# Second context attention: four row groups of scores at once, values a batch later, context loads behind the first gathers

## The reference

```python
    scale = 1.0 / jnp.sqrt(jnp.sqrt(jnp.float32(d)))
    q = x.reshape(B, T, H, d) * scale          # x is layer-normed; d = 16, H = 16
    k = cond_k.reshape(B, S, H, d) * scale     # cond_k = cond_v = ctx, S = 256
    w = jax.nn.softmax(jnp.einsum('bthd,bshd->bhts', q, k), axis=-1)
    out = jnp.einsum('bhts,bshd->bthd', w, v).reshape(B, T, W)
    return out @ w_proj.T + b_proj
```

## Time and profile before

| | |
|---|---|
| runs | 967.45 us median (965.89 to 968.01) |
| profiled execution, in all | 957.07 us |
| its span, first to last instruction | 955.2 us |
| mean granted TensorE clock | 0.909 |
| stage a2 in the trace | 667 to 802 us |
| PE busy over the span | 823.5 us (86%) |
| DVE, ACT, POOL busy | 586.8, 422.4, 329.7 us |

### The profile page before, as it was taken

How to read it: one execution, slowest core, us unless ns; L and a number is a source line. 1 busy time by engine, 2 the same in 40 slices (tenths; PEclk the granted TensorE clock), 3 DMA queues, 4 the chain that set the end, 5 groups by cost and what they waited for, 6 DMA issues and landing times. The chain is left out here.

```text
span 955.2 us, 20462 instructions
## 1 busy us (share of the span) xinstructions
PE 823.5 (86%) x7532; PEld 631.2 (66%) x7532; DVE 586.8 (61%) x1436; ACT 422.4 (44%) x1243; POOL 329.7 (35%) x465
## 2 busy tenths in 40 slices
PE   5999998898999999958787399998388996867897
PEld 4888887455999999834465388887266774465335
DVE  3555565446999999873495623223578787455474
ACT  3665655446654442023554210000257664555562
POOL 2112211113999999610051260100643332233001
PEclk9999999788999999875988599999589998979899
DMA  7112600000000000000001036532645210000001
GB/s 245 32 24 73 228 24 2 2 0 1 1 1 2 1 1 1 1 0 0 1 2 45 22 120 184 192 112 78 192 116 167 78 60 2 1 3 2 0 1 46
DMA packets 41846, 49.32 MB, mean 52 GB/s; under 512 B 7090, under 2 KB 37268, under 8 KB 41492
## 3 DMA queue, kind: packets, MB, share of 16 engines
q1 hardware_dynamic: 37204, 40.93, 13.4%
q0 software_dynamic: 1536, 4.20, 1.5%
q10 hardware_dynamic: 3008, 2.88, 0.9%
HBM read 43.81 MB, written 4.19 MB: 50 GB/s over the span
## 5 line engine op out<-in xcount | busy, mean ns | idle before, releaser
L723 POOL TENSOR_TENSOR r_faded<-r_state,rec_f 128x256 f32<-128x256 f32 x128 | 82.1, 642 | 19.8 <-DVE r_state L705 9.7
L751 PE MATMUL r_u_ps<-r_t_in,l_same_head 128*128 128x256 f32 x256 | 87.2, 422 | 0.1
L729 POOL TENSOR_TENSOR r_q_in<-r_state,rec_q 128x256 f32<-128x256 f32 x128 | 82.0, 641 | 0.3 <-DVE r_state L702 0.2
L758 PEld LDWEIGHTS r_o_ps<-l_head_of,r_q_in 128*128 128x128 f32 x512 | 77.0, 191 | 6.9 <-POOL r_q_in L729 0.4
L1428 ACT ACTIVATE a_prob<-a_s_ps,a_negmax 128x256 f32<-128x256 f32 x128 | 59.0, 488 | 38.3 <-DVE a_negmax L1465 38.2
L1088 ACT ACTIVATE a_prob<-a_s_ps,a_negmax 128x256 f32<-128x256 f32 x128 | 59.1, 486 | 19.0 <-DVE a_negmax L1144 19.0
L758 PE MATMUL r_o_ps<-l_head_of,r_q_in 128*128 128x8 f32 x512 | 65.2, 236 | 0.3 <-POOL r_q_in L729 0.3
L1651 POOL TENSOR_TENSOR a_prob<-a_prob,a_rden 128x512 f32<-128x512 f32 x32 | 32.3, 1042 | 84.5 <-DVE a_rden L1712 84.5
L1977 PE MATMUL m_h_ps<-m_rowsT,l_w 128*128 128x256 f32 x256 | 57.3, 383 | 0.0
L702 DVE TENSOR_TENSOR r_state<-r_update,r_faded 128x256 f32<-128x256 f32 x128 | 54.3, 424 | 4.4
L691 DVE TENSOR_TENSOR r_t_in<-r_state,r_par_ps 128x256 f32<-128x256 f32 x128 | 53.7, 420 | 5.3
(11 more groups left out here) (344 smaller groups left out, 1934.2 us busy)
## 6 DMA issues: line engine op xcount, KB each, us to landing
l_w<-in_B_w SPq DMA_DIRECT2D x16, 1024.0 KB, 5.6
a_ctxT<-in_ctxT SPq DMA_DIRECT2D x31, 256.0 KB, 2.8
a_ctx<-in_ctx SPq DMA_DIRECT2D x16, 256.0 KB, 3.6
expert_out<-m_y ACTq DMA_DIRECT2D x7, 256.0 KB, 5.7
all_X<-in_x SPq DMA_DIRECT2D x4, 256.0 KB, 5.6
l_b<-in_B_b SPq DMA_DIRECT2D x1, 1024.0 KB
routed_rows<-ffn_xn SPq DMA_DIRECT2D x8, 128.0 KB, 1.8
l_F_up<-in_F_up SPq DMA_DIRECT2D x1, 1024.0 KB, 6.1
```

Of the source, the lines that this page charges most:

```text
L723: nc.gpsimd.tensor_tensor(faded[m][:, :, :], state[(t + 1) % 2][m][:, :, :], row("f", t, m), ALU.mult).then_inc(faded_ready[m], 1)
L729: nc.gpsimd.tensor_tensor(q_in[t % 2][m][:, :, :], state[t % 2][m][:, :, :], row("q", t, m), ALU.mult).then_inc(q_ready[m], 1)
L751: nc.tensor.matmul(u_ps[t % 2][m][:, 0:B, :], same_head[:, :], t_in[m][:, :, :], start=False, stop=True).then_inc(u_mm[m], 1)
L758: mm = nc.tensor.matmul(o_ps[:, 2 * m + c, :, t % U], q_in[t % 2][m][:, c * (B // 2):(c + 1) * (B // 2), :], head_of[:, :], start=True, st ...
```

## The change

The scores of a batch become one group of 16 instructions over all four row groups, issued when all exponentials of the batch before are done. On PE the loop body for batch n becomes: scores(n+1), transposes 2 and 3 of n, values(n-1), output (odd n), the turn, transposes 0 and 1 of n+1. The list `uses` follows. ScalarE empties the banks of r = 0 and 1 before the next batch's exponentials; DVE those of r = 2 and 3, between and behind the maxima of the next batch, with heads and add behind them.

At the start, SP sends only the first `ctxT` and then waits for the first four combinings (`used`) before any other context load. The first queries are made by DVE straight from the turned bank in PSUM, four instructions (`first_queries`), instead of by POOL from `QT`; POOL issues the gathers 8 to 11 at once. DVE combines tile 2 ahead of the first queries and tile 3 behind them, takes the maxima of batch 0, then norms tiles 2 and 3 and lays out the values of batches 0 and 1 (`lay_out`). In the diff, lines without a change are left out where they don't help.

```diff
@@ -1230,7 +1230,7 @@
         normed = Normed(nc, sc, "x", X, eps, keep=sc.sb("x_rows", [P, NT, D]))
-        used, turned, turned_taken, first_values = (sc.sem(n) for n in ("used", "turned", "turned_taken", "first_values"))
+        used, turned, turned_taken, first_values, first_q = (sc.sem(n) for n in ("used", "turned", "turned_taken", "first_values", "first_q"))
         s_ps = [sc.ps(f"s_ps{r}", [P, KD, S]) for r in range(4)]
@@ -1244,17 +1244,18 @@
 
-            return (pt_act, ONE + n + 1) if r == 3 else (pt_dve, ONE + 3 * n + r + 1)
-        uses = [(("turned", 0), (turned_taken, ONE + 1))]
+            return (pt_act, ONE + 2 * n + r + 1) if r < 2 else (pt_dve, ONE + 2 * n + r - 1)
+        uses = [(("turned", 0), (turned_taken, ONE + 1))] + [((0, r), transposed(0, r)) for r in (0, 1)]
         for n in range(B):
-            for r in range(4):
-                uses.append(((n, r), transposed(n, r)))
-                if r == 1 and n % 2 == 1 and n > 1:
-                    uses.append((("out", n // 2 - 1), (x_added, ONE + n // 2)))
-                if r == 1 and n in TURNED_BESIDE:
-                    uses.append((("turned", TURNED_BESIDE[n]), (turned_taken, ONE + TURNED_BESIDE[n] + 1)))
+            uses += [((n, r), transposed(n, r)) for r in (2, 3)]
+            if n % 2 == 1 and n > 1:
+                uses.append((("out", n // 2 - 1), (x_added, ONE + n // 2)))
+            if n in TURNED_BESIDE:
+                uses.append((("turned", TURNED_BESIDE[n]), (turned_taken, ONE + TURNED_BESIDE[n] + 1)))
+            if n + 1 < B:
+                uses += [((n + 1, r), transposed(n + 1, r)) for r in (0, 1)]
         uses.append((("out", NT - 1), (x_added, ONE + NT)))
@@ -1274,6 +1275,8 @@
                     sp.dma_start(ctxT[n % NB][:, :, :], ctxT_d[n].rearrange("(k p) s -> p k s", p=P)).then_inc(ctxT_in[n % NB], 16)
+                    if n == 0:
+                        sp.wait_ge(used, ONE + 4)
                     if n >= NB:
@@ -1319,7 +1322,6 @@
                     gather(n)
-                queries(0)
                 for n in range(8, 12):
@@ -1338,19 +1340,20 @@
                     u = place[what]
+                    if u == 3:
+                        pe.wait_ge(first_q, ONE + 2 * KD)
                     if u >= 3:
...
 
-                def scores(n, h):
+                def scores(n):
                     t, j = n // 2, n % 2
-                    if h == 0:
-                        pe.wait_ge(q_ready, ONE + 2 * t + 2)
-                        pe.wait_ge(*loaded(ctxT_in, n))
+                    pe.wait_ge(*((q_ready, ONE + 2 * t) if t >= 1 else (first_q, ONE + 2 * KD)))
+                    pe.wait_ge(*loaded(ctxT_in, n))
                     if n >= 1:
-                        pe.wait_ge(exp_done, ONE + 4 * (n - 1) + 2 * h + 2)
+                        pe.wait_ge(exp_done, ONE + 4 * n)
                     for m in range(KD):
-                        for r in (2 * h, 2 * h + 1):
+                        for r in range(4):
                             rows = slice(32 * r, 32 * r + 32)
@@ -1369,7 +1372,7 @@
                         pe.wait_ge(heads_ready, ONE + t)
-                    for r in (2, 3):
+                    for r in (1, 3):
                         pe.wait_ge(*transposed(n, r))
@@ -1398,23 +1401,23 @@
                 turn(0)
-                scores(0, 0)
-                scores(0, 1)
+                scores(0)
+                transposes(0, 0)
+                transposes(0, 1)
                 for n in range(B):
-                    transposes(n, 0)
+                    if n + 1 < B:
+                        scores(n + 1)
+                    transposes(n, 2)
+                    transposes(n, 3)
                     if n >= 1:
                         values(n - 1)
-                    transposes(n, 1)
                     if n % 2 == 1 and n > 1:
...
                     if n + 1 < B:
-                        scores(n + 1, 0)
-                    transposes(n, 2)
-                    transposes(n, 3)
-                    if n + 1 < B:
-                        scores(n + 1, 1)
+                        transposes(n + 1, 0)
+                        transposes(n + 1, 1)
                 values(B - 1)
@@ -1436,6 +1439,8 @@
                     act.wait_ge(turned, ONE + c + 1)
+                    if c == 0:
+                        act.wait_ge(first_q, ONE + 2 * KD)
                     nc.scalar.activation(QT[:, :, c * 2 * P:(c + 1) * 2 * P], bank(("turned", c))[:, :].rearrange("p (k q) -> p k q", k=KD), ACT.Copy).then_inc(turned_taken, 1)
@@ -1444,14 +1449,13 @@
                 for n in range(B):
+                    for r in (0, 1):
+                        take_transposed(n, r)
                     if n + 1 < B:
-                        exps(n + 1, 0)
+                        for r in range(4):
+                            exps(n + 1, r)
                     if n in TURNED_BESIDE:
                         take_turned(TURNED_BESIDE[n])
-                    take_transposed(n, 3)
-                    if n + 1 < B:
-                        for r in range(1, 4):
-                            exps(n + 1, r)
                     if n == 3:
@@ -1503,35 +1507,47 @@
 
+                def lay_out(n):
+                    dve.wait_ge(*loaded(ctx_in, n))
+                    for e in range(2):
+                        nc.vector.tensor_copy(vals[n][:, e, :, :, e * HD:(e + 1) * HD], ctx[n][:, :, :].rearrange("p c (i e d) -> p c i e d", e=2, d=HD)[:, :, :, e, :]).then_inc(first_values, 1)
+                def first_queries():
+                    dve.wait_ge(turned, ONE + 1)
+                    for e in range(2):
+                        for k in range(KD):
+                            nc.vector.tensor_scalar(qpair[0][:, k, :, e, :], bank(("turned", 0))[:, 2 * k * P:(2 * k + 1) * P].rearrange("p (j q) -> p j q", j=2), par_q[:, e:e + 1], None, ALU.mult).then_inc(first_q, 1)
                 for j in range(2):
...
                 dve.wait_ge(zeroed, ONE + 2)
-                for n in range(2):
-                    dve.wait_ge(*loaded(ctx_in, n))
-                    for e in range(2):
-                        nc.vector.tensor_copy(vals[n][:, e, :, :, e * HD:(e + 1) * HD], ctx[n][:, :, :].rearrange("p c (i e d) -> p c i e d", e=2, d=HD)[:, :, :, e, :]).then_inc(first_values, 1)
-                for c in range(2):
-                    combine(2 * c)
-                    combine(2 * c + 1)
-                    normed.variances(dve, c)
-                    scale_tiles(c)
+                combine(0)
+                combine(1)
+                normed.variances(dve, 0)
+                scale_tiles(0)
+                combine(2)
+                first_queries()
+                combine(3)
+                normed.variances(dve, 1)
                 for r in range(4):
                     maxima(0, r)
+                scale_tiles(1)
+                lay_out(0)
+                lay_out(1)
                 for n in range(B):
-                    take_transposed(n, 0)
-                    if n >= 2 and n % 2 == 0:
-                        heads(n // 2 - 1)
-                    take_transposed(n, 1)
                     if n + 1 < B:
...
                         maxima(n + 1, 1)
-                    if n >= 3 and n % 2 == 1:
-                        add(n // 2 - 1)
                     take_transposed(n, 2)
-                    reciprocals(n)
                     if n + 1 < B:
...
                         maxima(n + 1, 3)
+                    take_transposed(n, 3)
+                    reciprocals(n)
+                    if n >= 2 and n % 2 == 0:
+                        heads(n // 2 - 1)
+                    if n >= 3 and n % 2 == 1:
+                        add(n // 2 - 1)
                     if n in (1, 2):
```

## The result

The changed kernel takes 951.18 us (median of 4 runs, 946.9 to 954.09), the kernel before beside it 966.79: ratio 0.984 with the interval 0.9815 to 0.9864, a gain of 15.6 us. The forecast was 956.9 with 953 to 964: the sign and the mechanism held, and the gain was larger than forecast. Three later measurements of such a pair, on three chips, gave 12.3 us (e5), 11.4 (e14) and 13.7 (e18).

A forecast was written before the change was run, and what follows sets the result against it. TensorE was taken to bound the later batches of the second context attention. Terms -6.8, -1.6, -3.35 and +1.2 summed to -10.55 us, taken off the 967.45 median to give 956.9, range 953 to 964.

The forecast's parts named there:

- 2, to the end of batch 0's exponentials: Stage start: batch 0's exponentials end at 688.4 instead of 689.96, -1.6 us (bounds +1.0 to -3.2).
- 4, tail: Stage end: batch 14's values and output 6 now also follow the last exponential, +1.2 us (0 to +2.4).
- the softmax loop: Steady batches: scores, maximum and eight exponentials through three engines bound each batch, sum 5.69 us, taken as 5.70.
- Rival A: Small gain: near-ties in the loop break, 6.0 instead of 5.7, start gives nothing; -3 to -7, 962 us; chance 0.24.
- rival D: Four row groups don't run together in this stage: scores 2.1, loop 6.75, sum +3, 970 us; chance 0.03.
- rival B: Larger gain: gathers land in 2.8 us throughout, tail costs nothing; -13.4, 954 us; chance 0.08.
- Rival C: Batch loop: TensorE idling drops the clock to 1.2 GHz, TensorE binds again; slower, 988 us; chance 0.06.
- Term 1: Batches 6 to 15: eight steps of 5.70 and two turned-tile steps of 6.65, 58.9 against 65.7 us, -6.8.
- Term 3: Batches 1 to 5: 36.75 against 40.1 us, -3.35, with the clock rise left at 699.
- if it rises at once, -1 to -2: Batches 1 to 5: an immediate clock rise would shorten them by a further 1 to 2 us.

The follow-up runs named there:

- e5: The changed kernel, unchanged, timed again beside the kernel before: 948.97 us beside 961.3, ratio 0.9867.
- e14: The changed kernel, unchanged, timed again in a pair with e13: 950.65 us, ratio 0.9876 to the kernel before.
- e18: The changed kernel, unchanged, timed again in a pair with e17: 947.43 us, ratio 0.9878 to the kernel before.
- e1: The kernel before, unchanged, timed and profiled again: 960.77 us beside 960.71, ratio 0.9993.
- e13: The kernel before, unchanged, timed and profiled again: 961.38 us beside 962.03, ratio 0.9994.
- e17: The kernel before, unchanged, timed and profiled again: 961.41 us beside 961.12, ratio 0.9998.
- e2: The changed kernel's batch loop with the start of the kernel before: 946.56 us beside 960.71 for the kernel before, ratio 0.986.
- e9: The changed kernel with scores cut into two halves of two row groups, a transposed group between: 956.75 us beside 966.5 for the kernel before, ratio 0.9899.
- e12: The changed kernel plus unread identity products, 43 ahead of the first turned tile, 17 behind the first scores: 952.14 us beside 966.5, ratio 0.9849.
- e11: The kernel before plus unread identity products, 50 ahead of the first turned tile, 10 behind the first scores: 966.53 us beside 966.5, ratio 1.0001.
- e10: The changed kernel with combinings spread over the first batches, gathers 12 to 15 earlier, batch 14's values moved forward: 947.59 us, ratio 0.9812 to the kernel before.
- e15: As e10 (spread combinings, earlier gathers, moved values), but without the hold of the context loads: 944.84 us beside 962.03 for the kernel before, ratio 0.9822.
- e8: The changed kernel plus unread identity products, 40 ahead of the first turned tile, 30 behind the first scores: 947.8 us beside 961.3, ratio 0.9866.
- e6: The changed kernel with its 16 score instructions ordered by row group: 947.24 us, ratio 0.9845 to the kernel before.

## Why the prediction was wrong in size

The stage by the prediction's terms, from the four profiles of each kernel unchanged (before: the first, e1, e13, e17; after: the first, e5, e14, e18):

| term | before, us | after, us | difference of means | first pair | forecast |
|---|---|---|---|---|---|
| 2, to the end of batch 0's exponentials | 21.93, 22.35, 22.63, 22.03 | 20.38, 21.00, 21.14, 21.57 | -1.2 | -1.55 | -1.6 |
| 3, batches 1 to 5 | 40.10, 40.68, 40.58, 39.59 | 38.04, 35.83, 35.82, 35.83 | -3.9 | -2.06 | -3.35 |
| 1, batches 6 to 15 | 65.73, 67.27, 67.27, 67.28 | 58.08, 59.66, 59.60, 58.09 | -8.0 | -7.65 | -6.8 |
| 4, tail | 6.51, 7.29, 7.37, 6.51 | 7.92, 7.92, 7.92, 7.91 | +1.0 | +1.41 | +1.2 |
| stage | 134.27, 137.59, 137.85, 135.41 | 124.42, 124.41, 124.48, 123.40 | -12.1 | -9.85 | -10.55 |

**Right.** The mechanism and its bound: the softmax loop of 5.77 us (5.70), the 16 scores in 1.08, TensorE idle in front of them. Rival A's ties cost nothing in this loop, rival D is refuted by each profile of the changed kernel, and of rival B neither cause held (the tail costs 1.0 to 1.4, and the exponentials of batch 0 gained 1.2 to 1.6). Rival C's fall of the clock came only as the single dips above, at most 1.6 us a stage in the changed kernel's four profiles. The steps forecast for batches 3 to 5, 7.3, 8.2 and 7.85, are 7.63, 7.88 and 7.84 (batch 3 of the first profile apart).

**Wrong, small.** Term 1: I gave two batches with a turned tile 6.65, for a wait of TensorE on the bank that the add frees. After's rows at batch 7, on PE and DVE:

```profile
734.84 1.04 PE L1367 MATMUL a_w_ps<-all_ident,a_prob 128*128 128x128 f32 x8
735.81 1.15 PE L1358 MATMUL a_s_ps<-a_ctxT,a_qpair 32*128 32x256 f32 x16
```

```profile
734.70 0.37 DVE L1494 TENSOR_TENSOR all_X<-a_w_ps,all_X 128x256 f32<-128x256 f32 x1
```

The add ends 5.35 us behind the last exponential before (729.72), not 5.6, and the transposes run through beside it: those steps are 5.98, TensorE's own work, 0.67 less each, 1.3 together; the eight others are 5.77 instead of 5.70, 0.5 more. Term 3: the clock rises about a batch earlier than I put it, so that step 2 is 5.76 and not 6.7; that was the prediction's own side condition ("if it rises at once, -1 to -2"). It stood in no case's sum.

**The step that failed.** "The median of the timed runs is 967.45, 10.4 longer than the profiled one; nothing says the difference lies in this stage, so I take the gain off it." Part of it does lie there. The first profile's stage of 134.27 is the shortest of four; the others are 1.1 to 3.6 us longer, at stretches with a granted clock under 1.00 around batch 6 or 7 and, in e1 and e13, at a later rise (step 2: 9.47 and 9.38 against 8.91 and, in e17, 8.02) and the tail (7.29 and 7.37 against 6.51, at a clock of 0.85 and 0.84 there). The old loop has TensorE as its bound in most of batches 6 to 15 and paid 1.5 us for its dip in each of the three later profiles; the changed kernel paid as much in e5 and e14 and nothing in the other two. So the change takes away more than one undisturbed execution shows: 12.1 us on the mean of four, where the sum from one gave 10.55. The kernel before accounts for 2.0 of that difference (mean 136.28 against 134.27), less 0.5 by which the changed one is longer than forecast (124.18 against 123.72). The pairs on a chip agree with it in time on average, though each is up to 2 us off: stage -13.4 and 11.4 us timed (e13, e14), -12.0 and 13.7 (e17, e18), -14.2 and 14.2 (e1, and e2 with the loop alone).

Of the 5.7 us between forecast and result, that is 1.5; 0.7 is the kernel before, at 966.79 in the second measurement instead of 967.45; the other 3.5 are the 15.6 us of the first measurement against 12.1. The interval of those 15.6 begins at 13.1 (966.79 x (1 - 0.9864)), so 2.5 of the 3.5 may be noise. They stay open. The kernel before took 966.5 to 966.8 us in two measurements (the first, and that of e9 to e12) and 960.7 to 962.0 in the four others, and idle times that nothing released stand in profiles of those two. For their costing the old order more: e11, the kernel before but for its added products, loses some 6 us to them in step 2, where the changed kernel lost 2.2 in its first profile and e12 0.7, in the values of the same batch; and with e11's stage as the old order's, e9 and e12 come out by stage as they do by time. Against its being all of it: nearly the same kernels gained 18.9 us there (e10) and 17.2 elsewhere (e15), 14.4 there (e12) and 13.5 elsewhere (e8), so 1 to 2 us more. It is not shown: there is no profile of the unchanged kernel before from a measurement in which its profile, too, took 966 us.

## What to carry to other kernels

Before a forecast from one profile is set on the median, ask whether the two differ, and let the sum have a term for it where the changed stage is bound by the engine whose clock varies. A change that takes TensorE off the path takes off what its clock costs only where another engine covers it: here batch 5 at 0.78 cost nothing, batches 6 and 7 still 1.5 us. When an engine is relieved, work out the next loop through the other engines link by link; here three links read from rows and one estimated gave 5.69 for a measured 5.77. And look for the last engine that has several pieces in a row where the others wait: spreading four combinings took 3.7 us off two steps, while the whole rearranged start gave nothing measurable.

## What the runs showed of the hardware

- The order within the 16 score instructions over four row groups doesn't matter: 1.08 us with the groups taken in turn, 1.10 with four of one group behind each other (e6). Two groups at a time cost 1.06 for eight instructions (e9), so the second pair is free only if it goes out in the same run.
- Short dips of the granted clock come in some executions of the same program and not in others (batch 6 of the kernel before: 8.09 or 9.62 us). In batches 6 and 7 a dip cost 1.5 us in either order, 0.94 of it where the scores are a link of the loop (e14); beside a stretch bound by VectorE or ScalarE it cost nothing (batch 4 of e14 at 0.66, batch 5 of e18 at 0.78).
- Idle times that nothing in the profile released: 0.42 to 0.52 us each, in e11 and e12 also one of 1.1 to 1.2, in a run of small matmuls (the changed kernel's first profile, e11, e12), and 2.88 on VectorE in front of a maximum whose scores had ended 7.7 us before (e10). The label "issue" also stands in front of ordinary waits: 8.51 us on ScalarE in e12, where VectorE's moments ended 0.04 us before.
